# Moving edge-row sends from the first convolution to the four recurrent blocks

## The chip, the cores and the metric

One core of one Trainium2 chip runs the whole program. The metric is the device time of one execution in microseconds (us). The engines are TensorE (PE: matrix products, with PEld for its weight loads), VectorE (DVE), ScalarE (ACT), GpSimd (POOL) and SyncE (SP). SP and POOL both issue DMAs here. The change concerns only DMAs that POOL issues.

## What is computed

Four graph layers run one after the other on 3125 nodes and 100000 edges. Each adds its result to its input and normalizes it:

```python
x = _layernorm(x + _L0_gnn_ref(x, edge_index, ...))      # two GIN convolutions
x = _layernorm(x + _L1_gnn_ref(x, edge_index, ...))      # two attention convolutions
x = _layernorm(x + _L2_gnn_ref(x, src, dst, ...))        # four GCN + GRU blocks
x = _layernorm(x + _L3_gnn_ref(x, edge_attr_64, src, dst, ...))

def _L3_gnn_ref(h, rbf_ij, idx_i, idx_j, W1, b1, W2, b2, W3, b3, W4, b4):
    W = jax.nn.silu(rbf_ij @ W1 + b1) @ W2 + b2
    msgs = h[idx_j] * W
    agg = jnp.zeros((n_atoms, h.shape[1]), dtype=h.dtype).at[idx_i].add(msgs)
    delta = jax.nn.silu(agg @ W3 + b3) @ W4 + b4
    return h + delta
```

The last layer sums messages by source node, while the edges come ordered by destination. So its input rows (64 attributes and two indices of each edge) have first to be put into the order of the source tiles. That can be done at any time before the last layer, and it depends on nothing that the first three layers compute.

## The kernel before

The program is a row of stages, each a function with a block of its own in which every engine has its own instruction stream. A stage ends when all engines have come to the end of the block. Then come a barrier, the clearing of the stage's semaphores and another barrier (`Mem.clear`, line 81, called through the `with` of each stage), and only then does the next stage issue anything. The order of stages is: `make_constants`, `edge_order` (which works out the place of each edge row), `build_counts` (a 3200 x 3200 matrix of edge counts), `gin_conv` "g0" and `gin_conv` "g1" (the first layer), `edge_tables`, two attention stages, `softmax_norm`, four times `gru_block`, `edge_messages` and `node_update`.

The edge rows are put in order beside other work, by a `Sender` (line 1720 on) on POOL's stream. The 782 chunks of 128 edge rows are shared out in order among the stages: 168 in `build_counts`, 150 in g0, 32 in `edge_tables` and 108 in each of the four `gru_block`s. What the short description of the change calls a batch of edge rows is one such chunk, and one send: an indirect DMA (line 1756) that writes 128 rows of 66 floats to 128 rows of the tensor `sorted`. In the code, and from here on in this text, a batch is a group of `size` chunks, loaded together (line 1737) into one of two buffers. For each batch POOL waits for the load (line 1748), copies the batch's indices (line 1749), drains, and issues its sends; halfway through it waits until the sends out of the other buffer have landed and issues the load of the next batch into it. At the end of the stage it waits for all sends to land (`end`, line 1769). g0 has 10 batches of 15 sends, each `gru_block` 12 batches of 9.

Beside that, `gin_conv` and `gru_block` have the same shape. First the source is loaded and split into bfloat16 parts (`Split`; lines 314 to 345). Then five groups of 640 nodes follow, each on a chain of PE (`sum_neighbours`, line 370, 150 matmuls, then the small products), ACT and DVE, and SP stores each group (line 446 in `gin_conv`, line 1487 in `gru_block`) and waits at the end for the last store to land (lines 447 and 1488). The barrier at a block's end is recorded at the line of the block's `with` (line 420 in `gin_conv`, line 1469 in `gru_block`) and those of `Mem.clear` at lines 84 and 86. g0 also stores the count matrix to HBM (line 439, `kept`, five DMAs of 4000 KB), and g1 has no sends.

Of the kernel before, what the change touches and what calls it, by code (L numbers as in the profile page):

```python
# [14 lines left out]
NT = -(-N_NODES // P)  # L15
# [524 lines left out]
def edge_tables(nc, K, D):  # L540
# [5 lines left out]
    with ExitStack() as ctx:  # L546
# [19 lines left out]
        bound = m.sb("p_bound", [1, NT + 1])  # L566
        sender = Sender(m, D, "p", *TABLE_SENDS)
        boundi = m.sb("p_boundi", [1, NT + 1], I32)
# [873 lines left out]
def gru_block(nc, K, D, AT, b, source, from_scale, to_scale, parts, target, residual):  # L1442

    with ExitStack() as ctx:
# [11 lines left out]
        split = Split(m, source, 1, parts, [work[:, i, :].rearrange("p (t c) -> p t c", c=P) for i in range(3)], from_scale)  # L1456
        sender = Sender(m, D, "r", *GRU_SENDS[b])
        y = m.sb("r_y", [P, GT, P])
# [132 lines left out]
NEAR_STEPS = 4  # L1591
ROWW = RBF + 2
COUNT_SENDS = (0, 7, NT - 1)
GIN_SENDS = (7 * (NT - 1), 15, 10)
TABLE_SENDS = (7 * (NT - 1) + 150, 16, 2)
GRU_SENDS = [(7 * (NT - 1) + 182 + 108 * b, 9, 12) for b in range(4)]
NSC = 7 * (NT - 1) + 182 + 432
SROWS = (NGRP + 1) * EGRP
FILL = (NGRP + 1) * SUB // 11
assert FILL * 11 == (NGRP + 1) * SUB and NGRP % NEAR_STEPS == 0 and NSC == NC  # L1600


def edge_order(nc, K, D):
# [4 lines left out]
    with ExitStack() as ctx:  # L1608
# [14 lines left out]
        offset = m.sb("o_offset", [P, NT])  # L1623
        slot = m.sb("o_slot", [P, NSC], I32)
        src_tile = m.sb("o_src_tile", [1, NHALF + HALVES], I32)
# [419 lines left out]
def gnn_program(nc, D):  # L2045

    def scratch(name, shape, dt=F32):
        D[name] = nc.dram_tensor(name, shape, dt, kind="Internal").ap()
# [19 lines left out]
    scratch("sorted", [SROWS, ROWW])  # L2068
    scratch("slot", [P, NSC], I32)
    scratch("src_tile", [1, NHALF + HALVES], I32)  # L2070
    scratch("tile_base", [P, NHALF])

    with ExitStack() as ctx:
# [6 lines left out]
        with ExitStack() as ctx2:  # L2080
            AT = Mem(nc, ctx2).sb("gin_counts", [P, NT, NP], BF16)
            build_counts(nc, K, D, AT)
            gin_conv(nc, K, D, AT, "g0", D["x"], 1, D["L0_W1a"], D["L0_b1a"], D["L0_W2a"], D["L0_b2a"], 2 * P,
                     D["gin1"], None, sends=GIN_SENDS, keep=D["kept"])
            gin_conv(nc, K, D, AT, "g1", D["gin1"], 2, D["L0_W1b"], D["L0_b1b"], D["L0_W2b"], D["L0_b2b"], P,
# [25 lines left out]
def laid_out(inputs):  # L2111
# [5 lines left out]
    def edges(v, fill, chunks):  # L2117
        full = np.full(chunks * P, fill, v.dtype)
        full[:E] = v
        return full  # L2120
# [12 lines left out]
    src, dst = edges(a["src"], NP - 1, NC), edges(a["dst"], PAD_DST, NC)  # L2133
    edge_rows = np.zeros(((NSC + 16) * P, ROWW), np.float32)
    edge_rows[:E, 0:RBF] = a["edge_attr_64"]
    edge_rows[:, RBF] = edges(a["src"], NP - 1, NSC + 16)
    edge_rows[:, RBF + 1] = edges(a["dst"], 0, NSC + 16).astype(np.int32).view(np.float32)
    out = {
# [42 lines left out]
```

How the kernel before makes its waits and increments, by code:

```python
            @block.gpsimd  # L115
            def _(pool):
                pool.iota(tile_edge[:, :], pattern=[[P, NT + 1]], base=0, channel_multiplier=0,
                          allow_small_or_imprecise_dtypes=True)
                pool.iota(edge[:, :], pattern=[[WIN, NWIN + 1]], base=0, channel_multiplier=0,
                          allow_small_or_imprecise_dtypes=True).then_inc(ready, 1)
                pool.iota(wins[:, :], pattern=[[1, NWIN + 1]], base=0, channel_multiplier=0,
                          allow_small_or_imprecise_dtypes=True).then_inc(ready, 1)
                pool.memset(K["identf"][:, :], 0.0).then_inc(ready, 1)
                pool.wait_ge(ready, 3)
                pool.affine_select(out=K["identf"][:, :], in_=K["identf"][:, :], compare_op=ALU.not_equal,
                                   fill=1.0, base=0, pattern=[[-1, P]], channel_multiplier=1).then_inc(ready, 1)
# [1 line left out]
            @block.vector  # L128
            def _(dve):
                dve.memset(ones[:, :], 1.0)
                dve.wait_ge(loaded, 32)
                dve.tensor_copy(lastf[:, :], last[:, :])
                dve.tensor_copy(farf[:, :], far[:, :])
                dve.drain()
                dve.wait_ge(ready, 2)
                for k in range(LASTS):
                    dve.tensor_scalar(over[:, k, :], edge[:, :], lastf[:, k:k + 1], None, ALU.is_gt)
                for k in range(FARS):
# [838 lines left out]
    def when(eng, sem, n):  # L977
        if not isinstance(n, int) or n > 0:
            eng.wait_ge(sem, n)
```

## Time and profile before

| | us |
|---|---|
| median of 3 runs | 6281.32 |
| lowest and highest run | 6271.79, 6281.51 |
| span of the profiled execution | 6282.4 |

The profiled execution's span, from its first to its last instruction, is all that is known of its own time. It lies 1.1 us above the median of the timed runs.

Busy over the span: PE 4259.3 us (68%), DVE 3797.3 (60%), POOL 3528.6 (56%), PEld 2971.7 (47%), ACT 1047.3 (17%). These shares are means over some fifteen stages with different limits, and none of them says what a send costs. Stages are separated by barriers, so a stage is as long as the slowest of its streams, and the profile has to be read stage by stage: at the end of each, which stream comes last, and how long the others have waited.

### The profile page before, as it was taken

How to read it: one execution, taken by the hardware profiler on the slowest of the kernel's cores; microseconds unless marked ns; L12 is line 12 of the kernel's file. 1: busy time of each engine (PE TensorE's matmuls, PEld its weight loads, DVE VectorE, ACT ScalarE, POOL GpSimd, SP SyncE). 2: the span in 40 equal slices, each digit the busy share in tenths (PEclk: the TensorE clock that was granted, in tenths of full speed). 3: DMA queues.
4: the chain of work that ended last, by engine and by line, in shares of the span. 5: the costliest groups of instructions: out<-in, count | busy, mean ns of one | idle time of the engine just before them, and what ended most of it. 6: DMA issues, size and time to landing. Idle time of an engine off the chain costs nothing. (4 is left out here: it accounts for less than half of the span.)

```text
span 6282.4 us, 102133 instructions
## 1 busy us (share of the span) xinstructions
PE 4259.3 (68%) x26578; PEld 2971.7 (47%) x26579; DVE 3797.3 (60%) x8630; ACT 1047.3 (17%) x1871; POOL 3528.6 (56%) x3626
## 2 busy tenths in 40 slices
PE   3666667395267777776256666666787777788884
PEld 1111115263156565655245555554454555566663
DVE  8777772154589999998456666666211235555553
ACT  0111111102211111111211111111211222222221
POOL 1222224502377777774277777771666667777771
PEclk9999999697589999998567777777898888988885
DMA  4000004201244444442333233334212222222233
GB/s 197 15 12 15 15 12 187 70 15 36 71 128 119 124 118 125 117 126 79 129 82 81 75 82 81 81 76 155 60 55 63 70 71 78 78 78 77 78 78 40
DMA packets 331742, 510.88 MB, mean 81 GB/s; under 512 B 104053, under 2 KB 245407, under 8 KB 321686
## 3 DMA queue, kind: packets, MB, share of 16 engines
q0 software_dynamic: 129376, 287.12, 17.6%
q1 hardware_dynamic: 202166, 221.78, 10.9%
q14 instruction: 158, 1.29, 0.1%
q8 instruction: 42, 0.69, 0.0%
HBM read 406.76 MB, written 101.86 MB: 81 GB/s over the span
## 5 line engine op out<-in xcount | busy, mean ns | idle before, releaser
L1061 POOL DMA_INDIRECT e_ring<-att_rows,e_near x1760 | 1791.3, 1018 | 553.7 <-issue 473.8
L1130 PE MATMUL e_psum<-e_ring,e_whole_pick 128*128 128x264 f32 (+1 forms) x3520 | 840.6, 392 | 244.5 <-DVE e_ring L1295 238.7
L1839 POOL DMA_INDIRECT e_nodes<-x,e_edges x832 | 808.6, 972 | 266.3 <-issue 239.2
L1130 PEld LDWEIGHTS e_psum<-e_ring,e_whole_pick 128*128 128x128 f32 x3520 | 643.6, 227 | 369.5 <-issue 175.8
L1085 PE MATMUL e_px<-t_parts,e_pick 128*128 x5280 | 671.9, 268 | 102.0 <-DVE e_pick L1193 51.5
L1209 DVE TENSOR_TENSOR e_prod<-e_px,e_ring 128x512 f32<-128x512 f32 x660 | 449.9, 682 | 386.8 <-DMA e_ring<-att_rows,e_near 277.4
L285 PE MATMUL b_acc<-b_pick_key,b_pick_lo 128*128 128x416 bf16 (+1 forms) x1960 | 495.9, 341 | 169.9 <-DVE b_pick_key L256 151.6
L1756 POOL DMA_INDIRECT sorted<-rx_held,rx_index x432 | 425.1, 984 | 220.4 <-issue 209.4
L1085 PEld LDWEIGHTS e_px<-t_parts,e_pick 128*128 128x128 bf16 x5280 | 442.8, 107 | 188.7 <-issue 119.2
L1173 ACT ACTIVATE e_whole_pick<-e_pturn 128x512 f32<-128x512 bf16 x440 | 261.7, 595 | 1351.6 <-PE e_pturn L1121 1329.0
L256 DVE TENSOR_SCALAR b_pick_key<-b_lane,b_base,b_keyf 128x800 bf16<-128x800 int16 x980 | 477.1, 487 | 0.0
L1199 DVE TENSOR_REDUCE e_dots<-e_prod 128x8 f32<-128x512 f32 (+1 forms) x660 | 444.8, 674 | 0.0
L1295 DVE TENSOR_TENSOR e_ring<-e_ring 128x1024 f32<-128x1024 f32 (+1 forms) x440 | 416.1, 946 | 26.7 <-issue 26.7
L1876 PE MATMUL e_pa<-e_msg,e_pick 128*128 128x128 f32 x1672 | 296.4, 332 | 191.5 <-DVEq L1938 191.2
L1876 PEld LDWEIGHTS e_pa<-e_msg,e_pick 128*128 128x128 f32 x1672 | 248.6, 228 | 362.7 <-DVEq L1938 355.2
L255 DVE TENSOR_SCALAR b_pick_lo<-b_lane,b_lof 128x128 bf16<-128x128 int16 x980 | 255.7, 261 | 236.8 <-PE b_acc L285 192.7
L370 PE MATMUL g_pa<-gin_counts,g_parts 128*128 x2250 | 312.7, 302 | 120.4 <-DMA g_b<-in_L_b2b 101.9
L285 PEld LDWEIGHTS b_acc<-b_pick_key,b_pick_lo 128*128 128x128 bf16 x1960 | 120.2, 97 | 529.9 <-DVE b_pick_key L256 514.9
L1946 DVE TENSOR_TENSOR agg<-agg,e_pa 128x128 f32 x418 | 120.5, 288 | 381.6 <-PE e_pa L1876 234.5
L209 POOL TENSOR_TENSOR gin_counts<-gin_counts,identb 128x128 bf16 (+1 forms) x25 | 12.7, 507 | 568.9 <-ACT gin_counts L266 568.9
L1089 PE MATMUL e_pside<-t_side,e_pick 128*128 x1760 | 332.1, 189 | 0.0
L370 PEld LDWEIGHTS g_pa<-gin_counts,g_parts 128*128 128x128 bf16 x2250 | 221.1, 99 | 211.9 <-issue 123.5
(348 smaller groups left out, 6766.7 us busy)
## 6 DMA issues: line engine op xcount, KB each, us to landing
e_relb<-place SPq DMA_DIRECT2D x56, 1024.0 KB, 6.0
e_ring<-att_rows,e_near POOLq DMA_INDIRECT x1760, 2.6
sorted<-o_fill SPq DMA_DIRECT2D x11, 2508.0 KB
e_edges<-sorted SPq DMA_DIRECT2D x209, 132.0 KB
kept<-gin_counts SPq DMA_DIRECT2D x5, 4000.0 KB
rx_held<-in_edge_rows POOLq DMA_DIRECT2D x52, 297.0 KB
e_nodes<-x,e_edges POOLq DMA_INDIRECT x832
gru_late<-kept SPq DMA_DIRECT2D x3, 4000.0 KB, 32.6
```

The costliest lines, as they stand in the source:

```text
L256: dve.tensor_scalar(pick_key[:, b, :], lane[:, :], base[:, ds(w, 1)], keyf[:, ds(c, 1)], ALU.add, ALU.is_equal).then_inc(picked, 1)
L285: mm = pe.matmul(acc[q % 2][:, h, 0:z - a], pick_lo[:, b, :], pick_key[:, b, a:z], start=False, stop=False, skip_group_check=True)
L370: mm = pe.matmul(banks, parts[:, k, j, f * P:(f + 1) * P], AT[:, j, ds(g * GW + half * HW, HW)], start=(j == 0 and k == 0), stop=(j == NT ...
L1061: pool.indirect_dma_start(out=ring[:, s, r, 0:wd + HEADS], out_offset=None, in_=xrows, in_offset=bass.IndirectOffsetOnAxis(ap=near[:, s, r ...
L1085: mm = pe.matmul(px[g % 2][:, x * wd:(x + 1) * wd], pick[:, 1 - s, r, :], parts[:, n, ds(t, 1), :].rearrange("p o c -> p (o c)"), start=(n ...
L1130: mm = pe.matmul(psum[q % 2][:, 0:RING], whole_pick[:, q % 2, c, :], ring[:, s, q * G + c, :], start=(c == 0), stop=(c == G - 1))
L1199: dve.tensor_reduce(dots[:, s, :, g * XB:(g + 1) * XB].rearrange("p h x -> p x h"), prod[:, g % 4, :].rearrange("p (x h c) -> p x h c", x= ...
L1209: dve.tensor_tensor(prod[:, g % 4, :].rearrange("p (x c) -> p x c", x=XB), px[g % 2][:, :].rearrange("p (x c) -> p x c", x=XB), ring[:, 1 ...
L1295: dve.tensor_tensor(rows_, rows_, ring[:, s, q * G:(q + 1) * G, wd:wd + HEADS].unsqueeze(3).broadcast_to([P, G, HEADS, ch]), ALU.mult).the ...
L1756: pool.indirect_dma_start(out=self.D["sorted"], in_=self.held[s][:, u, :], in_offset=None, out_offset=bass.IndirectOffsetOnAxis(ap=self.in ...
L1839: pool.indirect_dma_start(out=nodes[:, q, u, :], out_offset=None, in_=source, in_offset=bass.IndirectOffsetOnAxis(ap=edges[:, q, u, RBF + ...
L1876: mm = pe.matmul(pa[s][:, part * P:(part + 1) * P], pick[:, s, u, :], msg[:, s, u, :], start=(u % (SUB // HALVES) == 0), stop=(u % (SUB // ...
```

## The change

The table of who sends which chunks is altered, and nothing else. g0 sends 6 batches of 13 (78 chunks, 72 fewer), and each `gru_block` 14 batches of 9 (126 chunks, 18 more). The total stays 168 + 78 + 32 + 4 x 126 = 782.

```diff
 COUNT_SENDS = (0, 7, NT - 1)
-GIN_SENDS = (7 * (NT - 1), 15, 10)
-TABLE_SENDS = (7 * (NT - 1) + 150, 16, 2)
-GRU_SENDS = [(7 * (NT - 1) + 182 + 108 * b, 9, 12) for b in range(4)]
-NSC = 7 * (NT - 1) + 182 + 432
+GIN_SENDS = (7 * (NT - 1), 13, 6)
+TABLE_SENDS = (7 * (NT - 1) + 78, 16, 2)
+GRU_SENDS = [(7 * (NT - 1) + 110 + 126 * b, 9, 14) for b in range(4)]
+NSC = 7 * (NT - 1) + 110 + 504
```

The three numbers of an entry are the first chunk, the chunks of a batch and the number of batches.

## Rows read from the trace of the kernel before

**Rows 1.** Busy time of each engine by stretch; the first line names the columns.
```profile
core 0: us, PE busy (x) PEld busy (x) DVE busy (x) ACT busy (x) POOL busy (x), PEclk, DMA share, GB/s
...
1134.00:1236.00 102.00, 0.11 (x1) 0.12 (x2) 4.01 (x6) 3.97 (x6) 62.12 (x69) 0.51 0.21 61
976.00:1134.00 158.00, 141.91 (x890) 100.82 (x890) 23.38 (x44) 15.40 (x30) 92.09 (x100) 0.97 0.49 188
...
4545.00:4727.00 182.00, 141.95 (x855) 93.95 (x855) 31.96 (x67) 30.99 (x50) 117.61 (x134) 0.88 0.22 62
```
**Rows 2.** Waits of SP's queue at g0's end: line, cause, total us, times, longest.
```profile
SPq L420 <- PEq L420: 87.3, 1, 87.3
...
SPq L420 <- DMA gin<-g_y: 2.7, 1, 2.7
```
**Rows 3.** The same waits at the end of g1, which sends nothing.
```profile
SPq L420 <- DMA x<-g_y: 2.0, 1, 2.0
...
SPq L420 <- PEq L420: 0.2, 1, 0.2
```
**Rows 4.** The same wait for the barrier in recurrent blocks 1 to 4.
```profile
SPq L1469 <- PEq L1469: 5.0, 1, 5.0
...
SPq L1469 <- PEq L1469: 4.9, 1, 4.9
...
SPq L1469 <- PEq L1469: 6.6, 1, 6.6
...
SPq L1469 <- PEq L1469: 2.2, 1, 2.2
```
**Rows 5.** Timeline of SP from g0: start, us, queue, line, operation, tiles, count.
```profile
1013.16 122.78 SPq L446 DMA_DIRECT2D gin<-g_y  x5
1227.42 0.96 SPq L314 DMA_DIRECT2D g_hid<-gin  x2
```
**Rows 6.** Timeline of POOL in g0: first sends of batches 0, 1, 2, 9, and the last.
```profile
976.59 1.28 POOL L1756 DMA_INDIRECT sorted<-g0x_held,g0x_index  x1 [0.99 <-issue]
...
1026.04 0.98 POOL L1756 DMA_INDIRECT sorted<-g0x_held,g0x_index  x1 [19.09 <-issue]
...
1049.11 0.98 POOL L1756 DMA_INDIRECT sorted<-g0x_held,g0x_index  x1 [3.24 <-issue]
...
1204.02 0.98 POOL L1756 DMA_INDIRECT sorted<-g0x_held,g0x_index  x1 [2.48 <-issue]
...
1222.33 0.96 POOL L1756 DMA_INDIRECT sorted<-g0x_held,g0x_index  x1 [0.30 <-issue]
```
**Rows 7.** Timeline of POOL, block 1: first sends of batches 1 and 11, last send, next block.
```profile
4388.97 0.97 POOL L1756 DMA_INDIRECT sorted<-rx_held,rx_index  x1 [2.23 <-issue]
...
4530.67 0.98 POOL L1756 DMA_INDIRECT sorted<-rx_held,rx_index  x1 [2.42 <-issue]
...
4541.40 0.95 POOL L1756 DMA_INDIRECT sorted<-rx_held,rx_index  x1 [0.30 <-issue]
4546.38 0.57 POOL L1741 DMA_DIRECT2D rx_slot<-slot  x1 [4.03 <-POOLq L86]
```
**Rows 8.** Sends, ns min/median/max: 1136 to 1224, 1027 to 1134, 4370 to 4386 us.
```profile
L1756 POOL DMA_INDIRECT sorted<-g0x_held,g0x_index x60: 954/958/983, 1138.2 to 1222.3; - x60
...
L1756 POOL DMA_INDIRECT sorted<-g0x_held,g0x_index x74: 954/958/1452, 1026.0 to 1132.9; - x74
...
L1756 POOL DMA_INDIRECT sorted<-rx_held,rx_index x9: 954/1211/1526, 4372.8 to 4385.6; - x9
```
**Rows 9.** Matmuls of line 370 at the start of g1 and block 1, and block 1's timeline.
```profile
L370 PE MATMUL g_pa<-gin_counts,g_parts x16: 444/474/475, 1235.9 to 1239.9; 128*128 x16
...
L370 PE MATMUL g_pa<-gin_counts,g_parts x32: 299/300/475, 1239.6 to 1244.9; 128*128 x32
...
L370 PE MATMUL r_pa<-gru_early,gru_parts x29: 298/474/475, 4373.7 to 4379.9; 128*128 x29
...
4373.69 6.70 PE L370 MATMUL r_pa<-gru_early,gru_parts 128*128 x30 [17.01 <-ACT gru_parts L321]
```

## The prediction

> **What bounds the kernel now.** The page's shares of busy time don't help, since the program is a row of stages with a barrier after each. I therefore asked four things of the two kinds of stage that the change touches: how busy the engines are by stretch, what SP's queue waits for at a stage's end, when POOL's batches start, and how long single sends take.
>
> The busy times by stretch [rows 1] show g0 in two parts. From 976 to 1134 us PE works 141.9 of 158 us. From 1134 to 1236 us PE runs 0.11 us, DVE and ACT 4 us each, and POOL 62 us: for about 90 us POOL alone works. The recurrent blocks look different: in the 182 us of block 2, PE works 142 us and POOL's instructions take 118, so neither seems full. This is where a share of busy time misleads, because POOL's gaps between sends (0.30 us each) are not idle time that could be filled.
>
> The waits of SP's queue decide it. In each of these stages SP's last work is to wait for its last store, and after that it stands at the block's barrier until the slowest stream comes. In g1, which has no sends, the store lands after 2.0 us of waiting and the barrier then takes 0.2 us [rows 3]: the compute side ended that stage. In g0 the store takes 2.7 us and the barrier 87.3 us [rows 2]. The trace writes both barriers against PE's queue, but PE had done its last matmul by 1134 [rows 1]; what is still running is POOL, whose last send starts at 1222.33 [rows 6], and the next stage's first DMA is at 1227.42 [rows 5].
>
> In the four recurrent blocks the same wait is 5.0, 4.9, 6.6 and 2.2 us [rows 4]. This is the row that carries the forecast: it is not 0.2. **POOL is already the last stream in all four blocks.** In block 1 its last send is issued at 4541.40 and ends at 4542.35, and the next stage begins 4.03 us later [rows 7]. There is no slack there to take anything in.
>
> **What is removed from g0.** With 78 sends in 6 batches POOL ends earlier than the compute side. A batch of 15 takes (1204.02 - 1049.11) / 7 = 22.13 us from first send to first send [rows 6]. Sends within a batch start 0.96 + 0.30 = 1.26 us apart [rows 6, 7], so the rest of a batch (copy, drain, load) takes 22.13 - 15 x 1.26 = 3.2 us, and a batch of 13 takes 13 x 1.26 + 3.2 = 19.6 us. Batch 1 starts at 1026.04 only, after 19.09 us in which nothing that the profile shows held POOL [rows 6]; the five 4000 KB stores of the count matrix are then in flight. I leave that stall where it is, since smaller batches don't end those stores sooner; without it POOL would only be done still earlier. From there, batch 1 takes 23.07 us now [rows 6] and 2 x 1.26 less with two sends fewer, 20.5 us; batches 2, 3 and 4 take 19.6 each; so batch 5 starts at 1026.04 + 20.5 + 58.8 = 1105.3. Its 13 sends and the load take 12 x 1.26 + 0.6 + 0.96 = 16.7 us: the last send is issued by 1122.0.
>
> The last store of g0 is issued by 1013.16 + 122.78 = 1135.94 [rows 5] and waited for 2.7 us more [rows 2], to 1138.6. So POOL has some 14 us to spare (its last send also has to land, in perhaps the 2 to 3 us that stores take here), and the wait of 87.3 us falls to g1's 0.2. **The stage gets 87.1 us shorter.** That is the whole gain to be had: of the 3 batches or so of sends beyond this point that also go, nothing more comes back, since PE's chain now ends the stage. The bounds are these. If the stall at 1026 grew by more than the 14 us, each further us would be lost; I allow 7 us of loss. On the other side g1's start may be a little better, next paragraph.
>
> **TensorE's clock.** g1 starts after 102 us without matmuls, at the lower level: its first 16 matmuls take 474 ns where later ones take 299 [rows 9]. After the change the gap is about 15 us (1134 to 1140 + 8.5, the time from g1's first DMA to its first matmul [rows 5, 9]). But block 1 starts after a gap of 17.01 us and also begins at 474 ns [rows 9]. If g1 were spared all of its slow start, some 20 to 25 matmuls of 0.175 us, that would be 4 us; I take 0 and keep 4 for the range.
>
> **What is added to the recurrent blocks.** Each gets two more batches of 9, at the end of a stream that is already the last. In block 1 the ten batches from 1 to 10 take (4530.67 - 4388.97) / 10 = 14.17 us each [rows 7], with everything in it: one load issue, nine sends, the copy, the drain. Two batches are 28.3 us, and four blocks make 113.4 us. Below, a batch can't cost less than its parts: nine sends of 0.958 us, eight gaps of 0.30, the 2.23 us before a batch's first send and a load issue of 0.57 [rows 7, 8], without the copy, are 13.8 us, or 110.6 in all. Above, if the added ones were as slow as a block's first (nine sends of median 1.211 us instead of 0.958 [rows 8]), a batch would cost 2.3 us more, and all eight 18 us more.
>
> Nothing hides this. What waits for POOL at the barrier is everything: the next block loads its source (line 314) only after it, so PE, ACT and DVE stand still for 28.3 us more each time, and after block 4 the message stage does. The sends are issued on POOL alone, so no other queue is moved past. Their DMA traffic is light (62 GB/s in the whole stretch of block 2 [rows 1]), and the time that PE's longer pause costs in a colder start of the next block (under 0.175 us for each of some 30 matmuls, 5 us) is covered: the compute side will be ready 28.3 + 2 to 7 us before POOL in each block.
>
> One rule speaks of the place of the sends. In g0's lonely tail 60 sends take a median of 958 ns, and 74 sends beside PE, DVE and ACT take 958 as well, with a maximum of 1452; only the nine at a block's start, beside the splitting, have a median of 1211 [rows 8]. The Trainium skill ("SBUF — State Buffer", section "SBUF: two separate sides") says that while DVE runs an operation in a two-port mode GpSimd is locked out of the shared port and can't write its descriptors. By that rule a send is dearer beside DVE than alone, and moving 72 of them out of a tail in which DVE is silent would cost something of its own; the rows agree for the nine and not for the 74. Because streams are in order, the eighteen sends that a block gains lie behind DVE's last instruction whichever they are, so by the rule too they cost the plain price.
>
> **The sum.** 6282.4 (span) - 87.1 + 113.4 = 6308.7 us, that is +26.3. The span is 1.1 us above the median of the timed runs, so I predict 6281.3 + 26.3 = 6307.6 us. It is about +0.42%.
>
> **The rivals.**
> The blocks take it in: the added sends lie in a pause of POOL, and only g0's gain shows. That needs POOL to end a block at least 28 us ahead of the last store. It would give 6281.3 - 87.1 = 6194 us, faster by 1.4%. For it speaks only that POOL's instructions are busy 118 of 182 us [rows 1]; against it is each of the four waits in [rows 4]. 4%.
> The two sides cancel to within 12.6 us: g0 gives back more than its barrier wait, or the added batches are cheaper. Even with 4 us from the clock and 110.6 us of cost the sum is +19.5, so it needs a further 7 us, such as a gain from fewer transfers beside the splitting of g1, of which no row shows a sign. It would give about 6291. 7%.
> The sends are dear in their new place, as the rule on the shared port would have it if they fell beside DVE: 18 us more, +44, or 6326 us. It decides if the sends at the end of the blocks have a median near 1.2 us instead of 0.96. 5%.
> POOL still ends g0: the stall at 1026 lasts longer than 14 us beyond today's. With the stall doubled (19 us more) the stage would lose 5 us of the gain, 6313 us: inside the range, and nothing tells it from the forecast but the barrier wait of g0. 6%.
> That the change doesn't do what it says I can rule out by count: 78 + 504 = 582 = 150 + 432.
>
> **How the numbers follow.** The forecast itself has 78%. The terms leave 110.6 - 91.1 = +19.5 at the low end and, with 7 us lost in g0 and a batch of 14.35 us (the mean from a block's first send at 4372.8 on [rows 7, 8]), 114.8 - 80.1 = +34.7 at the high end, or 6301 to 6316. The runs of the kernel before spread over 10 us, mostly downwards. That makes 6293 to 6318, with the fourth rival inside and the others outside or at the edge. What a measurement of this kernel can tell from no change is about 0.2%, or 12.6 us. Slower by more than that: forecast, third and fourth rival, 89%. Within it: 7%. Faster: 4%.
>
> **What would show each step.** In the profile after, SP's barrier wait at the end of g0 should fall to under 1 us, POOL's last send there should be issued near 1122, and g1's first DMA should come near 1140. The waits at the end of the blocks should be 33, 33, 35 and 30 us, and each block should last 28 us longer; from 5093 us on everything should be shifted by 26 us and otherwise unchanged. The median send stays at 958 ns. The prediction is wrong if the waits at the end of the blocks grow by clearly less than 28 us, or if g0's wait keeps a part of its 87.

## The result and the profile after

| | before | after |
|---|---|---|
| median, us | 6281.32 | 6302.39 |
| ratio (95% interval) | 1 | 1.0039 (1.0025 to 1.0052) |
| span of the profiled execution, us | 6282.4 | 6297.8 |

One of the five timed runs of the changed kernel took 11006.8 us in a slower state of the chip, and it counts in the median of the table but in none of the ratios of this text, which are of undisturbed runs. The change makes the kernel slower, by 24.5 us if the ratio is taken (15.7 to 32.7 by its interval) and by 20.3 us by the medians with that run left out (6301.65 and 6281.32 us). The forecast was +26.3 us.

At the end of g0 SP's queue now waits as it does at the end of g1. These are its waits in the last 12 us of the stage (line, cause, us in total, times, longest), to be set beside [rows 2]:

```profile
SPq L420 <- DMA gin<-g_y: 2.7, 1, 2.7
...
SPq L420 <- PEq L420: 0.2, 1, 0.2
```

The 87.3 us are gone. At the ends of the four recurrent blocks the same wait, beside [rows 4], reads:

```profile
SPq L1469 <- PEq L1469: 33.1, 1, 33.1
...
SPq L1469 <- PEq L1469: 35.1, 1, 35.1
...
SPq L1469 <- PEq L1469: 33.3, 1, 33.3
...
SPq L1469 <- PEq L1469: 29.7, 1, 29.7
```

It has grown from 18.7 to 131.2 us in all: the wait that g0 had once is gone, and about a third of it (28 us) has been added four times. The busy times of one block and of the 37 us at its end show what it is made of (us and counts for PE, PEld, DVE, ACT and POOL, then TensorE's clock, DMA share and GB/s):

```profile
4477.00:4687.00 210.00, 139.98 (x855) 93.33 (x855) 32.07 (x67) 31.00 (x50) 135.82 (x156) 0.83 0.21 59
4650.00:4687.00 37.00, 0.00 (x0) 0.00 (x0) 0.00 (x0) 0.00 (x0) 23.12 (x27) 0.50 0.17 49
```

No other engine runs in these 37 us. PE's busy time in the block is 140 us, against 142 in [rows 1]; only the stage around it has grown, to 210 us. SP's timeline gives the starts of the stages, g1 and blocks 2, 3 and 4 (start, us, queue, line, operation, tiles, count); the second row answers to the last of [rows 5]:

```profile
1010.33 124.52 SPq L446 DMA_DIRECT2D gin<-g_y  x5
1139.19 0.96 SPq L314 DMA_DIRECT2D g_hid<-gin  x2
...
4477.14 1.52 SPq L314 DMA_DIRECT2D r_work<-state  x3
...
4687.27 1.53 SPq L314 DMA_DIRECT2D r_work<-state  x3
...
4898.10 1.53 SPq L314 DMA_DIRECT2D r_work<-state  x3
```

From such rows every stage's length can be taken, from its first DMA to the next stage's first (of a recurrent block to its first load of weights, 1.6 us later). The fifth column is the kernel of the experiments that has nothing changed.

| stage, us | before | after | difference | before, again |
|---|---|---|---|---|
| up to g0 | 966.8 | 967.9 | +1.2 | 966.1 |
| g0 | 260.7 | 171.3 | -89.4 | 260.9 |
| g1 | 275.2 | 272.0 | -3.2 | 274.6 |
| edge_tables | 73.4 | 73.4 | +0.1 | 73.8 |
| first attention | 1443.6 | 1443.7 | 0.0 | 1443.7 |
| second attention | 1284.8 | 1279.8 | -5.0 | 1281.3 |
| softmax_norm | 62.4 | 61.1 | -1.3 | 63.4 |
| block 1 | 180.7 | 209.6 | +28.8 | 179.5 |
| block 2 | 181.8 | 210.1 | +28.3 | 181.2 |
| block 3 | 182.5 | 210.8 | +28.3 | 180.9 |
| block 4 | 181.2 | 209.6 | +28.4 | 180.9 |
| messages, node update | 1189.3 | 1188.6 | -0.8 | 1188.4 |
| span | 6282.4 | 6297.8 | +15.4 | 6274.6 |

The stages that the change touches give -89.4 + 113.8 = +24.4 us. The other 9 us between that and the span's +15.4 lie in stages that it leaves alone.

### The profile page after: what moved, and what is told of

It reads as the page before. It is cut to its first block and busy times, and to the rows that moved or that the text cites. A ratio compares the mean times of both kernels' runs of the same rounds, so it can differ in the third digit from the quotient of the medians.

```text
span 6297.8 us, 102169 instructions
## 1 busy us (share of the span) xinstructions
PE 4224.5 (67%) x26578; PEld 2941.2 (47%) x26579; DVE 3796.0 (60%) x8630; ACT 1047.9 (17%) x1871; POOL 3522.9 (56%) x3634
## 5 line engine op out<-in xcount | busy, mean ns | idle before, releaser
L1756 POOL DMA_INDIRECT sorted<-rx_held,rx_index x504 | 493.9, 980 | 260.0 <-issue 247.5
L370 PE MATMUL r_pa<-gru_early,gru_parts 128*128 x1200 | 209.9, 344 | 180.6 <-DMA r_bh<-in_gru_bh 114.8
## 6 DMA issues: line engine op xcount, KB each, us to landing
gru_late<-kept SPq DMA_DIRECT2D x3, 4000.0 KB, 33.1
```

The source lines that it names most:

```text
L370: mm = pe.matmul(banks, parts[:, k, j, f * P:(f + 1) * P], AT[:, j, ds(g * GW + half * HW, HW)], start=(j == 0 and k == 0), stop=(j == NT ...
L1756: pool.indirect_dma_start(out=self.D["sorted"], in_=self.held[s][:, u, :], in_offset=None, out_offset=bass.IndirectOffsetOnAxis(ap=self.in ...
```

## Experiments

### g0's part alone

```diff
-GIN_SENDS = (7 * (NT - 1), 15, 10)
+GIN_SENDS = (7 * (NT - 1), 13, 6)
```

> The kernel before with only g0's part of the change: 6 batches of 13 sends instead of 10 of 15, nothing added elsewhere. 72 chunks of edge rows are sent by nobody, so the last layer's sum lacks them; the number of instructions in the other stages is the same. Theory (each stage is as long as its slowest stream, and each part of the change has its own price): SP's barrier wait at the end of g0 falls from 87.3 to about 0.2 us and the time by 87 us, to about 6194 (-1.39%), perhaps 3 us more since g1 starts with a less rested TensorE. The recurrent blocks keep their length of 181 to 183 us. Rival (the gain of g0 was larger than its barrier wait, and that is why the whole change cost less than forecast): 92 us or more fall away, 6189 or less, and the difference sits in g0 and g1. Rival (DMAs of g0 were of use to nobody but their absence lets later stages run otherwise): the stages behind g1 change by more than their own scatter.

Measured: median 6187.42 us, ratio 0.9852 (0.9837 to 0.9868) to the kernel before on the same chip, which is -93 us (-102 to -83). g0 lasts 173.3 us instead of 260.7, that is -87.3, and SP's barrier wait there is the row of the changed kernel once more:

```profile
SPq L420 <- PEq L420: 0.2, 1, 0.2
```

The stage gives back its barrier wait and no more, and the recurrent blocks keep 180.8 to 181.5 us. The whole time moved 6 us further than the stage, within the interval. In the profiled execution the surplus lies in the recurrent blocks, g1 and the second attention (272.5 and 1281.9 us), which have less than in the kernel before although nothing in them is changed. The first rival is thus half met: the time was lower than 6189, but not in g0. Of the second, no stage behind g1 shows a sign: the second attention, the one that moved most, lies between the two executions of the unchanged kernel (1281.3 and 1284.8).

### The blocks' part alone

```diff
-GRU_SENDS = [(7 * (NT - 1) + 182 + 108 * b, 9, 12) for b in range(4)]
+GRU_SENDS = [(7 * (NT - 1) + 164 + 108 * b, 9, 14) for b in range(4)]
```

> The kernel before with only the blocks' part of the change: 14 batches of 9 sends in each recurrent block instead of 12, g0 as it was. The 18 more chunks of each block are ones that were sent before and are sent a second time to the same places, so nothing is left out. Theory: POOL was the last stream in each block, so each gets 2 x 14.17 = 28.3 us longer and the time rises by 113 us, to about 6395 (+1.8%); SP's barrier waits at the block ends become about 33, 33, 35 and 30 us. Rival (the blocks take part of it in): the waits grow by less than 28 us and the time by clearly less than 113 us, say 95. Rival (sends beside other work are dear): over 125 us.

Measured: median 6391.41 us, ratio 1.0177 (1.0161 to 1.0194), or +111 us (101 to 122). The blocks last 209.4, 209.5, 211.6 and 210.0 us, together 114.2 us more than in the kernel before. g0 keeps its barrier wait, and the blocks' waits have grown by 28 us each (g0, then blocks 1 to 4):

```profile
SPq L420 <- PEq L420: 85.9, 1, 85.9
...
SPq L1469 <- PEq L1469: 33.1, 1, 33.1
...
SPq L1469 <- PEq L1469: 32.9, 1, 32.9
...
SPq L1469 <- PEq L1469: 33.8, 1, 33.8
...
SPq L1469 <- PEq L1469: 30.4, 1, 30.4
```

So the blocks take in nothing, and sends at their end aren't dear either. The two parts alone make -93 + 111 = +18 us, and the whole change made +24.5 (15.7 to 32.7): there is no effect of the one on the other that these intervals could tell.

### Fewer sends in the blocks

```diff
-GRU_SENDS = [(7 * (NT - 1) + 182 + 108 * b, 9, 12) for b in range(4)]
+GRU_SENDS = [(7 * (NT - 1) + 182 + 108 * b, 9, 10) for b in range(4)]
```

> The kernel before with 10 batches of 9 sends in each recurrent block instead of 12, g0 as it was; 72 chunks are sent by nobody, so the last layer's sum lacks them. It asks how far POOL leads or trails in the blocks. Theory: POOL's stream gets 28.3 us shorter in each block, but only the barrier wait of SP can be given back: 5.0 + 4.9 + 6.6 + 2.2 - 4 x 0.2 = 18 us in all, to about 6263 (-0.29%), and the waits fall to about 0.2. Rival (a send costs its 28.3 us wherever it stands, as it does upwards): -113 us, 6168. Rival (the blocks are bound by PE already and the wait that the trace shows is something else): no change.

Measured: median 6260.74 us, ratio 0.9972 (0.9962 to 0.9983), or -17.6 us (-24 to -11). The blocks last 175.5, 176.1, 175.6 and 180.0 us, 19.1 us less in all, and the waits at their end are those of a stage that the compute side ends (block 1; the other three read the same):

```profile
SPq L1469 <- DMA state<-r_y: 2.0, 1, 2.0
...
SPq L1469 <- PEq L1469: 0.2, 1, 0.2
```

This shows that the small waits of [rows 4] were the price of POOL being last, and not a barrier's own cost. Two batches more cost 28 us in each block; two batches fewer give back 5, 6, 7 and 1 us. The bend lies where the forecast put it, at the wait that SP had.

### The same 72 sends in build_counts

```diff
-COUNT_SENDS = (0, 7, NT - 1)
-GIN_SENDS = (7 * (NT - 1), 15, 10)
+COUNT_SENDS = (0, 10, NT - 1)
+GIN_SENDS = (10 * (NT - 1), 13, 6)
...
-GRU_SENDS = [(7 * (NT - 1) + 182 + 108 * b, 9, 12) for b in range(4)]
+GRU_SENDS = [(10 * (NT - 1) + 110 + 108 * b, 9, 12) for b in range(4)]
```

> The same 72 sends are taken from g0 as in the change, but given to build_counts instead: 24 batches of 10 sends there instead of 24 of 7, g0 6 batches of 13, the recurrent blocks as before. Nothing is left out. Theory: in build_counts POOL is busy a quarter of the time and waits each turn for ACT's counts, so three more sends per turn of some 35 us are hidden, and the time is that of the kernel with only g0's part: -87 us, about 6194 (-1.39%). Rival (a port that VectorE and GpSimd share: VectorE builds the one-hot rows there and ends each turn): each send that falls beside VectorE holds it up; with 0.25 us for each of 72 sends it would be 18 us less, about 6212, and build_counts would last that much longer than 850 us.

Measured: median 6192.02 us, ratio 0.9857 (0.9842 to 0.9873), -90 us. The busy times from 110 to 966 us, in the kernel before and in this one:

```profile
110.00:966.00 856.00, 565.12 (x2360) 150.85 (x2360) 609.58 (x1970) 121.91 (x225) 200.87 (x245) 0.98 0.05 15
```

```profile
110.00:966.00 856.00, 564.90 (x2360) 151.74 (x2360) 610.21 (x1970) 121.92 (x225) 271.31 (x317) 0.98 0.07 20
```

POOL has 70 us more of work, DVE's 1970 instructions take 0.6 us more in all, and g0 starts at 968.6 us instead of 966.8. Seventy-two sends are hidden here that cost 113 us in the blocks. The port rival (18 us more) is out at its size; a smaller effect on VectorE is taken up with the last of these kernels.

### Sends in g1

```diff
-GIN_SENDS = (7 * (NT - 1), 15, 10)
+GIN_SENDS = (7 * (NT - 1), 13, 6)
+G1_SENDS = (7 * (NT - 1) + 78, 2, 36)
...
-                     D["x1"], D["x"], outdeg=outdeg)
+                     D["x1"], D["x"], sends=G1_SENDS, outdeg=outdeg)
```

> The 72 sends that the change takes from g0 are given to g1, in 36 batches of 2 (no more room in SBUF), g0 has 6 batches of 13, the recurrent blocks are as before. Nothing is left out. Theory: g1 has 272 us in which POOL does nothing and its barrier wait is 0.2 us; 36 batches of some 6 us are about 215 us, so POOL ends first and the time is that of the kernel with only g0's part, about 6190 (-1.4%). Rival (short batches are dearer: each waits for its own load of about 3 us and for the landing of the sends before it, together over 7.5 us): POOL becomes the last stream of g1 and the barrier wait there rises over 0.2 us.

Measured: median 6190.34 us, ratio 0.9867 (0.9852 to 0.9882), -84 us (-93 to -74). The sends of g1 in this kernel (line 1757 there; ns min/median/max, first and last start):

```profile
L1757 POOL DMA_INDIRECT sorted<-g1x_held,g1x_index x72: 979/982/1484, 1145.6 to 1332.0; - x72
```

The last of the 36 batches begins at 1330.2 us, so a batch of two takes (1330.2 - 1145.6) / 35, or 5.3 us, and a send costs POOL 2.6 us instead of 1.6. It makes no difference, since POOL is done 79 us before the next stage begins (1412.2) and g1 keeps 272.9 us.

### The kernel before once more

> The kernel before once more, with the same instructions; only a comment in its source differs. It asks how far a stage's length and the whole time scatter with nothing changed, since the changed kernel lay about 11 us under the forecast on its span, in g1 (-3.2), the second attention (-5.0), softmax (-1.3) and g0 (-2.3), of which only g0 is touched by the change. Theory (that rest is scatter, and the profiled execution of the kernel before lay high): stages that nothing touches come out anywhere between the values seen so far, g1 272.0 to 275.3 us, second attention 1279.8 to 1284.8, and the ratio is 1.000. Rival (the change really makes these stages shorter): g1 near 275 and the second attention near 1285 again, and only kernels with the change have 272 and 1280.

Measured: ratio 0.9997 (0.9988 to 1.0006), span of the profiled execution 6274.6 us. That is 7.8 us below the profiled execution of the kernel before with the same instructions, which therefore lay high. Its second attention takes 1281.3 us and not 1284.8, and its four blocks 722.5 us and not 726.2: scatter. So do the small barrier waits of [rows 4], which are 4.1, 4.9, 4.9 and 1.5 us here. g1 is less clear. It takes 274.6 us here, and two rows of TensorE's timeline (line 471, five times in g1) show where 1.6 us come from:

```profile
1336.63 4.13 PE L471 MATMUL g_pa<-g_w,g_hid 128*128 128x128 f32 x20 [1.87 <-ACT g_hid L483]
...
1389.18 2.50 PE L471 MATMUL g_pa<-g_w,g_hid 128*128 128x128 f32 x20 [1.87 <-ACT g_hid L483]
```

The same 20 matmuls take 4.13 us once and 2.50 us at other times, and the granted clock of the 50 us around the slow group reads 0.97 where it is 1.00 in undisturbed ones. In a slow group itself (kernel before, 1439.5 to 1443.6 us) it reads 0.58, near the lower of TensorE's two levels (1.2 and 2.4 GHz), and 1.00 in the 3 us before and behind. Ahead of it PE had waited 1.87 us for ACT, but so it had ahead of the fast groups. One such group is in g1 of the kernel before (4.12), of this one and of the one with fewer sends in the blocks, and in none of the seven others. These three are the ones in which g1 begins at 1227 us; in the others it begins at 1225 or at 1139 to 1145. (The repeat has a second one, of 3.50 us.) Three and seven executions don't settle whether that is chance, and what lowers the clock there stays open. It is worth 1.6 to 3 us.

### Out of g0 and out of the blocks

```diff
-COUNT_SENDS = (0, 7, NT - 1)
-GIN_SENDS = (7 * (NT - 1), 15, 10)
+COUNT_SENDS = (0, 13, NT - 1)
+GIN_SENDS = (13 * (NT - 1), 13, 6)
...
-GRU_SENDS = [(7 * (NT - 1) + 182 + 108 * b, 9, 12) for b in range(4)]
+GRU_SENDS = [(13 * (NT - 1) + 110 + 90 * b, 9, 10) for b in range(4)]
```

> Sends are moved out of both kinds of stage in which POOL comes last: 24 batches of 13 in build_counts (312 chunks), 6 of 13 in g0, 10 of 9 in each recurrent block. Nothing is left out. Theory: the gains add, 87 to 90 us from g0 and 18 to 21 us from the blocks' barrier waits, to about 6173 (-1.72%), if build_counts hides six more sends in each turn than before, as it hid three. Rival (build_counts has no room left, or the load of its bigger batches is in the way): its stage gets longer than 857 us and the time stays near 6190.

Measured: median 6176.56 us, ratio 0.9841 (0.9828 to 0.9855), -100 us (-108 to -91). The ratio is 1.6% short of 1 where the expectation had 1.72%, which is the edge of the interval (1.45 to 1.72%). The blocks last 175.2, 176.3, 175.5 and 180.1 us and all barrier waits are 0.2 us. g0 starts at 972.0 us, 5 us later than before, so the rival's sign, a stage of more than 857 us, is there (860 us from its first DMA, against 855). Whether the sends in build_counts have a part in that isn't settled, but in the next kernel, with 24 sends more in that stage, g0 starts at 966.7, so it isn't their number.

### Few sends in edge_tables too

```diff
+COUNT_SENDS = (0, 14, NT - 1)
+GIN_SENDS = (14 * (NT - 1), 14, 6)
+TABLE_SENDS = (14 * (NT - 1) + 84, 1, 2)
+GRU_SENDS = [(14 * (NT - 1) + 86 + 90 * b, 9, 10) for b in range(4)]
```

> As the kernel with both moved, and edge_tables keeps only 2 of its 32 sends; build_counts has 24 batches of 14, g0 6 of 14. Nothing is left out. It asks whether sends hold up VectorE: in edge_tables they take a median of 1212 ns instead of 958, beside VectorE's work on tables. Theory (a send is slowed beside some of VectorE's instructions, but VectorE is not held up by the send, and POOL is not the last stream there): edge_tables keeps its 73.4 us, and the time is that of the kernel with both moved within 2 us. Rival (a port that both share also holds up VectorE): edge_tables gets shorter by 30 x 0.25 = 7.5 us, to about 66 us.

Measured: median 6170.09 us, ratio 0.9833 (0.9818 to 0.9848), the lowest of all. The expectation had it within 2 us of the kernel with both moved, and that was missed: it is 6.5 us lower, with no overlap of the runs (6166.9 to 6173.3 us against 6174.1 to 6178.6). Between the two profiled executions 5.3 us lie ahead of g0, 3.5 in the first attention and 2.7 in softmax_norm, and nothing in edge_tables, which keeps its length (73.3 us). Its longest group of VectorE instructions, with 32 sends beside it (kernel before) and with 2 (this kernel):

```profile
L633 DVE TENSOR_SCALAR p_rel<-p_dst x25: 626/627/636, 1518.8 to 1555.7; - x25
```

```profile
L633 DVE TENSOR_SCALAR p_rel<-p_dst x25: 626/627/628, 1427.2 to 1464.2; - x25
```

This group is not held up by sends. The sends themselves take a median of 1212 ns in that stage of the kernel before, and POOL's timeline there shows where: from about the start of this group of VectorE's to about its end, but neither before it, when ScalarE was already at work, nor behind it.

```profile
1518.47 1.03 POOL L1756 DMA_INDIRECT sorted<-px_held,px_index  x1 [0.30 <-issue]
1519.81 1.24 POOL L1756 DMA_INDIRECT sorted<-px_held,px_index  x1 [0.30 <-issue]
...
1555.25 1.23 POOL L1756 DMA_INDIRECT sorted<-px_held,px_index  x1 [0.30 <-issue]
...
1558.23 0.96 POOL L1756 DMA_INDIRECT sorted<-px_held,px_index  x1 [0.30 <-issue]
```

ScalarE's row of instructions there runs from 1508.1 to 1550.7 us, so the sends are slow with VectorE's group and not with ScalarE's: the seven ahead of the group, beside ScalarE, take 0.95 to 1.07 us, and the last five in it, with ScalarE done, 1.15 to 1.23.

In build_counts the effect goes the other way too, though it is small. These are VectorE's two main groups there (number of instructions, us in all, mean ns), first with 168 sends beside them (kernel before) and then with 336 (this kernel):

```profile
L256 DVE TENSOR_SCALAR b_pick_key<-b_lane,b_base,b_keyf 128x800 bf16<-128x800 int16 x980 | 477.1, 487 | 0.0
L255 DVE TENSOR_SCALAR b_pick_lo<-b_lane,b_lof 128x128 bf16<-128x128 int16 x980 | 255.7, 261 | 236.8 <-PE b_acc L285 192.7
```

```profile
L256 DVE TENSOR_SCALAR b_pick_key<-b_lane,b_base,b_keyf 128x800 bf16<-128x800 int16 x980 | 482.7, 493 | 0.0
L255 DVE TENSOR_SCALAR b_pick_lo<-b_lane,b_lof 128x128 bf16<-128x128 int16 x980 | 260.9, 266 | 230.4 <-PE b_acc L285 185.9
```

Together they take 731.5 to 733.2 us in the seven profiled executions with 168 sends, 734.8 with 240, 741.1 with 312 and 743.6 with 336. That is some 0.06 us for each send more, a quarter of the rival's 0.25 (the batches and their loads grow with the sends, so that these aren't told apart), and in this kernel it does not lengthen the stage: g0 starts at 966.7 us, as in the kernel before.

## Why the prediction was right

**What ends each stage.** Right, and the whole forecast hung on it. The forecast read POOL's place from the wait of SP's queue at a stage's end, 87.3 us in g0 and 5.0, 4.9, 6.6 and 2.2 us in the blocks, against 0.2 us in a stage without sends. Taking two batches out of the blocks turned these four waits into 0.2 and gave 19.1 us by stages, against 18.7 - 0.8 = 17.9 us by the rows.

**g0.** Forecast -87.1 us, measured -89.4 (change) and -87.3 (g0's part alone). The barrier wait fell to 0.2 us as forecast and g1 starts at 1139.2 instead of "near 1140". POOL was done sooner than worked out: its last sends are

```profile
1112.98 0.96 POOL L1756 DMA_INDIRECT sorted<-g0x_held,g0x_index  x1 [0.31 <-issue]
1114.24 0.96 POOL L1756 DMA_INDIRECT sorted<-g0x_held,g0x_index  x1 [0.30 <-issue]
```

and the forecast had the end at 1122.0. The step that was off is the one that left the stall where it was, because the stores of the count matrix would not end sooner. The start of batch 1 moved from 1026.04 [rows 6] to

```profile
1020.01 0.98 POOL L1756 DMA_INDIRECT sorted<-g0x_held,g0x_index  x1 [16.90 <-issue]
```

3.8 us of it because the load of the batch (13 chunks instead of 15) had landed earlier, and 2.2 because the stall itself was shorter, 16.90 us instead of 19.09. The stores did not end sooner: the DMA engines' share is 0.93 or more up to 1032 us in both kernels, beyond the end of the stall, so what ends it stays open. It costs nothing, as POOL was not the last stream in any case. The forecast also speaks of "3 batches or so" beyond the point where the compute side ends; 60 sends, four batches, began after 1138 us [rows 8], and of the 101 us that it takes off POOL's stream some 14 bring nothing. No term of the sum rests on that.

**The blocks.** Forecast +28.3 us each, 113.4 in all; measured 28.8, 28.3, 28.3 and 28.4, or 113.8. The end of POOL's stream in block 2 has the pattern of [rows 7]: the first sends of its last two batches, the last send, and the next block's first DMA on POOL's queue:

```profile
4657.88 0.98 POOL L1756 DMA_INDIRECT sorted<-rx_held,rx_index  x1 [2.22 <-issue]
...
4671.98 0.97 POOL L1756 DMA_INDIRECT sorted<-rx_held,rx_index  x1 [2.22 <-issue]
...
4682.71 0.96 POOL L1756 DMA_INDIRECT sorted<-rx_held,rx_index  x1 [0.30 <-issue]
4687.70 0.57 POOL L1741 DMA_DIRECT2D rx_slot<-slot  x1 [4.03 <-POOLq L86]
```

The last two batches start 14.10 us apart, the sends in them take 958 ns (median of the last 29), and the way from the end of the last send to the next block is 4.03 us as before. The waits were forecast at 33, 33, 35 and 30 us and came at 33.1, 35.1, 33.3 and 29.7, that is 28.1, 30.2, 26.7 and 27.5 us more. They scatter more than the blocks' lengths, since a wait also depends on when the compute side ends.

**TensorE's clock.** The forecast took nothing for the shorter pause ahead of g1. g1's first 300 matmuls take 42.67 us after a pause of 14.36 us, and 43.84 and 42.28 us (the kernel before and its repeat) after one of over 101 us: no difference to be told, as assumed. A colder start of the blocks, which the forecast had hidden behind POOL, did not come: the first 30 matmuls of block 2 take 5.53 us after a pause of 47.83 us and took 6.39 us after one of 19.96, and PE's busy time in the block is 140 us where it was 142, while the stage is 28 us longer.

**The rule on the shared port.** The Trainium skill ("SBUF — State Buffer", section "SBUF: two separate sides") has GpSimd and VectorE lock each other out when VectorE runs a two-port operation. As forecast, the end-of-block sends take 958 ns, behind VectorE's last instruction. Where the two work side by side, the trace agrees in part. In edge_tables sends take 1.2 us for just as long as one group of VectorE's runs, but that group itself is not slower for them (627 ns with 32 sends and with 2); in build_counts VectorE's two main groups take 11 us more with 168 sends more. Which of these are two-port operations no run shows, and an engine that stands still for the whole of the other's instruction is seen in neither stage.

**What was off.** The sum was 2 to 6 us too high against the timed runs, and 11 us against the spans. (The message stage begins 16 us later in the profiled execution, where the forecast had a shift of 26.) Of these 11 us, g0 has 2.3, and the rest is in stages that nothing touches. The term behind it is the base: the span of a single execution, which lay 7.8 us above that of a second execution of the same instructions. Against that second one the touched stages come to (171.3 - 260.9) + (840.1 - 722.5) = +28.0 us, and the forecast of 26.3 lies between this and the 24.4 of the first.

**The rivals.** That the blocks take the sends in (6194 us) is out by their lengths. That the two sides cancel is out by the interval, though the sum of the parts measured alone (+18) lay only some 5 us above the 12.6 that bound that rival. Dear sends in the new place and a stall that keeps POOL last in g0 are out by the rows above.

## What to carry to other kernels

Where stages are divided by barriers, look at how long the other queues stand at the barrier, and not at an engine's busy share: POOL was busy for 118 of 182 us in the blocks and still last by 5 us. Work moved from a stream that is 87 us late to four streams that are already a few us late costs its full length in each of them, and gives back only the lateness that it removes from the first. The same 72 sends were free in two stages that POOL did not end and in which it had long pauses: g1, whose barrier wait was 0.2 us, and build_counts, where with the 72 more POOL's last send begins at 925.9 us, 43 us before the next stage. And 6170 to 6177 us was reached by moving work away from every stage in which POOL came last.

## What the runs showed of the hardware

A send of 128 rows costs POOL 1.26 us from start to start in g0 and the blocks, outside their first sends, and the batch costs about 3 us on top (14.17 us for nine, 22.13 for fifteen, 5.3 for two), so a send comes to 1.57, 1.48 and 2.6 us. Beside one group of VectorE's instructions in edge_tables the same send takes 1.2 us instead of 0.96, and in build_counts VectorE's two main groups were 1.5% longer with twice as many sends (743.6 us instead of 731.5 to 733.2). TensorE's clock can fall for a few us (to a reading of 0.58) in a stretch in which PE is busy 47 of 50 us: the same 20 matmuls took 4.13 and 2.50 us within one stage. And the time of one execution scatters by some 10 us without any change (the eleven runs of the repeat lie between 6270.1 and 6280.5 us). The two attention stages, which nothing in these kernels touches, have lengths between 1440.7 and 1446.8 and between 1279.8 and 1284.8 us in ten profiled executions.
